# Clearing the semaphores of each stage inside the following stage instead of in a step of its own

## What is computed

```python
x = _layernorm(x + _L0_gnn_ref(x, edge_index, W1, b1, W2, b2))          # two graph convolutions
x = _layernorm(x + _L1_gnn_ref(x, edge_index, edge_type_8, W, root, bias))  # mean for each of 8 edge types
x = _layernorm(x + _L2_gnn_ref(x, W, edge_index, edge_type_8))          # attention, softmax over an edge type
x = _layernorm(x + _L3_gnn_ref(x, weight, edge_index, edge_type_16))    # sum for each of 16 edge types, relu
```

## Time and profile before

| | us |
|---|---|
| median of 3 runs | 3187.77 |
| lowest, highest | 3186.46, 3187.91 |
| profiled execution, its time | 3188.55 |
| profiled execution, span from first to last instruction | 3186.8 |
| mean granted TensorE clock in it | 0.854 |
| busy PE, DVE, ACT, POOL | 2283.0, 2338.2, 1719.3, 2111.0 |

### The profile page before, as it was taken

The page is one execution under the profiler, slowest core; times in us unless marked ns, Lnnn a source line. Parts: engine busy times, 40 slices in busy tenths (PEclk is TensorE's granted clock), DMA queues, the critical chain, the costliest instruction groups (busy, mean ns, idle before and its releaser), DMA issues. The chain is left out here.

```text
span 3186.8 us, 51629 instructions
## 1 busy us (share of the span) xinstructions
PE 2283.0 (72%) x9863; PEld 1461.5 (46%) x9864; DVE 2338.2 (73%) x7354; ACT 1719.3 (54%) x4736; POOL 2111.0 (66%) x2070
## 2 busy tenths in 40 slices
PE   2666661777746666599999576577645499999996
PEld 1444441666645666344444333366534355444442
DVE  7999982788859889599999211133489678899996
ACT  1776892898947777466666344455458512121221
POOL 1777776777547777477776677577540277677775
PEclk9998996999978788799999699755555599999998
DMA  1666672455536666355554587799745423222221
GB/s 49 216 214 199 205 219 75 151 177 172 167 108 188 192 184 186 118 148 150 151 157 148 174 269 267 223 284 288 232 128 175 138 70 73 63 60 62 62 63 38
DMA packets 320188, 497.19 MB, mean 156 GB/s; under 512 B 65930, under 2 KB 144681, under 8 KB 320058
## 3 DMA queue, kind: packets, MB, share of 16 engines
q1 hardware_dynamic: 251130, 379.68, 37.3%
q0 software_dynamic: 68928, 116.12, 13.8%
HBM read 262.91 MB, written 236.52 MB: 157 GB/s over the span
## 5 line engine op out<-in xcount | busy, mean ns | idle before, releaser
L2156 PE MATMUL bank<-sum_masked,sum_w 128*128 128x512 f32 x1280 | 568.5, 596 | 6.7 <-DVE sum_masked L2215 6.7
L2215 DVE SCALAR_TENSOR_TENSOR sum_masked<-sum_typ,sum_col 128x512 f32<-128x512 bf16 x640 | 401.5, 684 | 21.0 <-ACT sum_col L2131 17.5
L1381 PE MATMUL bank<-mean_masked,mean_w 128*128 128x512 f32 x784 | 376.7, 612 | 18.7 <-DVE mean_masked L1472 18.7
L2156 PEld LDWEIGHTS bank<-sum_masked,sum_w 128*128 128x128 f32 x1280 | 236.5, 191 | 281.3 <-issue 210.1
L2075 POOL DMA_INDIRECT sum_rows<-t_x,m_row_int x160 | 171.7, 1073 | 197.2 <-POOLq L122 148.8
L2097 POOL DMA_INDIRECT out_dram<-sum_new,m_last_int x196 | 220.9, 1127 | 88.0 <-issue 57.8
L1237 POOL DMA_INDIRECT mean_rows<-t_x,m_row_int x196 | 213.8, 1091 | 95.5 <-issue 95.5
L1472 DVE SCALAR_TENSOR_TENSOR mean_masked<-mean_typ,mean_col 128x512 f32<-128x512 bf16 x392 | 250.0, 680 | 20.8 <-ACT mean_col L1317 20.7
L1237 POOL DMA_INDIRECT c_rows<-t_g,m_row_int x196 | 188.7, 963 | 109.7 <-issue 56.7
L1698 POOL DMA_INDIRECT at_xs<-t_x,at_order x204 | 193.6, 949 | 94.3 <-issue 60.7
L1248 POOL DMA_INDIRECT order<-m_row_int,m_order_int x196 | 213.0, 1087 | 59.7 <-issue 59.7
(11 more groups left out here) (366 smaller groups left out, 6039.0 us busy)
## 6 DMA issues: line engine op xcount, KB each, us to landing
t_hu<-at_made SPq DMA_DIRECT2D x51, 512.0 KB, 3.7
pf_xc<-x_dram SPq DMA_DIRECT2D x98, 256.0 KB
t_g<-pf_g SPq DMA_DIRECT2D x98, 256.0 KB
t_x<-pf_x SPq DMA_DIRECT2D x98, 256.0 KB
c_dense_x<-t_x SPq DMA_DIRECT2D x98, 256.0 KB, 3.8
t_x<-c_dense_x SPq DMA_DIRECT2D x98, 256.0 KB
c_same<-p_same SPq DMA_DIRECT2D x98, 128.0 KB, 3.5
t_g<-c_new SPq DMA_DIRECT2D x49, 256.0 KB
```

Source lines behind the costliest of these rows:

```text
L1381: pe.matmul(H[q][:, :], w[:, r, :], masked[:, r % MASKS, :], start=(r == 0), stop=(r == n_rel - 1))\
L2156: pe.matmul(H[n % 2][:, :], w[:, r * D:(r + 1) * D], masked[:, r % 8, :], start=(r == 0), stop=(r == R16 - 1)).then_inc(mask_used, 1)
L2215: v.scalar_tensor_tensor(out=masked[:, r % 8, :], in0=typ[:, n % 2, :], scalar=float(r), in1=col[:, n % 2, :], op0=ALU.is_equal, op1=ALU.m ...
```

## The change

The second Block behind each stage goes. A stage's exit now calls `finish`, which emits no instruction: it gives back the semaphores of the stage before (already cleared by then) and notes its own as `m.finished`. Each following stage has `clear_finished(pool, m)` in GpSimd's list. One Block with `clear_finished` stands behind sum.

```diff
-    def clear(self):
-        with self.nc.Block() as block:
-            @block.gpsimd
-            def _(pool):
-                for s in self.mine:
-                    pool.sem_clear(s)
-        for s in self.mine:
+    def finish(self, m):
+
+        for s in m.finished:
             self.nc.release_semaphore(s)
+        m.finished = self.mine
+
+
+def clear_finished(pool, m):
+
+    for s in m.finished:
+        pool.sem_clear(s)
...
-        ctx.callback(sem.clear)
+        ctx.callback(sem.finish, m)
         block = ctx.enter_context(nc.Block())
...
+            clear_finished(pool, m)
             with pool.If(out_of_order(pool)):
...
+
+        @block.gpsimd
+        def _(pool):
+            clear_finished(pool, m)
...
                 gather_info(pool, m, k)
+            clear_finished(pool, m)
             hold(pool, gathered, KT * 16)
             hold(pool, m.info_gathered, (KT - INFO_LATE) * 16)
...
+            clear_finished(pool, m)
             if kind == ATTEND:
                 for z in range(KZ):
...
+            clear_finished(pool, m)
             for q in range(4):
                 pool.wait_ge(scattered[q], of_four(NB - 1 - (NB - 1 - q) % 4, q, 16 * BT))
...
     m = Memory()
+    m.finished = []
...
         sum_stage(nc, io, m)
+        with nc.Block() as block:
+            @block.gpsimd
+            def _(pool):
+                clear_finished(pool, m)
```

## The result

The kernel after takes 3158.89 us (median of 5 runs, 3155.18 to 3161.65), the kernel before 3187.72 on the same chip (5 runs, 3185.77 to 3187.91). The ratio is 0.9911, with an interval of 0.9897 to 0.9925: 28.8 us less, where 22.4 were forecast.

A forecast was written before the change was run, and what follows sets the result against it. No engine is busy over 73%, so eleven stages run in a row, with clearing steps in series between them. 3187.77 - 22.4 for ten steps, moved clears and late starts at 0, gives 3165.4 us; 8-in-10 range 3162.8 to 3173.4.

The forecast's parts named there:

- The removed steps: Ten of the eleven clearing steps between two barriers behind the stages go, saving their full length, 22.4 us.
- The count of clears: Cross-check of the ten steps: 288 clears at 0.065 us plus ten drains and barriers at 0.3 us, together 21.7 us.
- The clears at nothing: 288 clears moved into GpSimd's lists in the stages add 0 us; upper bound 2.3 us.
- The rival in which clears wait for the DMAs: Clears queue until GpSimd's DMAs are worked off, in attention and sum: 2.3 us given back, 3167.7; chance 0.05.
- What is late next: Start of the next stage's list behind each barrier: 0 us taken, at most 2.0 to 3.5 us for one boundary.
- the rivals in which the steps were cover for code: Boundaries stall on code loads: four give back 8 to 14 us, chance 0.13; all ten cost 35 us, chance 0.03.
- The argument against code loads: In prefill's step nobody stopped for the instruction load there, as the 38 clears kept their pitch.
- the range's lower end: Whole kernel: 3162.8 us, from known executions of the kernel before lying 2.1 us below.

The follow-up runs named there:

- empty_step: The kernel after with the ten second Blocks put back without their clears, each one drain and one barrier: 3167.93 us, ratio 0.9932 to the kernel before.
- pool_first: The kernel after with prefill's 12 clears at the head of GpSimd's list instead of behind the gathers: 3163.53 us.
- pool_pad12: The kernel after with 12 drains added to GpSimd's list in setup: 3167.89 us.
- second set: Both kernels run again unaltered: the kernel after 3160.75 us against 3189.18 for the kernel before, ratio 0.9912.
- dve_pad18: The kernel after with 18 drains at the head of VectorE's list in ATTEND: 3166.06 us, one run.
- before_ranges: The kernel before, second Blocks kept, with each step's clears written as clears of semaphore ranges, 26 instructions instead of 313: 3168.84 us, ratio 0.9937.
- pool_pad21: The kernel after with 21 drains added to GpSimd's list in setup: 3154.28 us, one run.

## Why the prediction was right, and where it was short

- **The removed steps: right.** 22.4 us were forecast, 22.26 measured. The count of clears (21.7) was the worse of the two ways, as it put a barrier at 0.3 us; empty_step shows 0.33.
- **The clears at nothing: right, by the reason given.** The sequencer runs ahead: sum's 37 clears were over at 3142.2, when GpSimd still had 6 us of scatters to do; the drain behind them took 4.615 us, against 4.625. The rival in which clears wait for the DMAs, 2.3 us, is out. In attention, where I gave it 1.8 us of cover, the stage is as long as before within its scatter (532.2 and 531.7 against 532.1 and 530.3).
- **What is late next: right for the ten boundaries, and too narrow a question.** SP's first load comes 0.07 us behind the release that is left at eight boundaries and 0.26 behind that of constants, as it did before; softmax has none. So the rivals in which the steps were cover for code, 8 to 35 us back, are out, although one such wait can be made: pool_first and pool_pad12 have 3.6 and 3.7 us. I asked this only as a possible cost ("bounded from below by nothing"). The value below nothing was excluded by the sentence that every boundary starts as prefill's does. It doesn't: the trace of before had GpSimd's first gather of prefill 2.3 us behind the release, with 1.45 us of "issue" in front, while behind prefill's own barrier and step the first gather came 0.8 us behind the release. The argument against code loads, that the 38 clears of prefill's step kept their pitch, was misread too: in the rows of setup, prefill, attention and ATTEND one gap is 0.36 to 0.44 us instead of 0.07, each with an instruction packet 0.7 us behind it.
- **The step that failed is the range's lower end, with the term "what is late next" held at nothing or more.** In its place the runs show 6.5 us (6.2 in the second set) that the stages themselves became shorter. The lower end was made of the scatter of before alone, 2.1 us, and even that was subtracted wrongly: 3165.4 - 2.1 is 3163.3 and not 3162.8. What it left out is that the removal shortens each engine's list, and that the trace of before holds waits that depend on the place in it or change for another reason. I had read the longest "issue" waits on VectorE and ScalarE, as a price for new ones; the same view has one of 4.8 us on GpSimd, in the stage that GpSimd bounds:

```profile
POOL m_xd L614 <- issue: 65.4, 196, 4.8
```

- **The excess, by its parts.** Of 6.5 us between the medians prefill gave 3.3 (4.3 in the second pair of profiled executions), VectorE's loop branch in ATTEND 8 x 0.21 = 1.7, and MEAN's passes 8 x 0.08 = 0.6: 5.6. The remaining 0.9 lies within the runs' scatter, and so does much of the sum, which only the medians give and not each pair of traces. That ATTEND's part is the place of VectorE's code is shown by dve_pad18, and by empty_step and before_ranges, which leave VectorE's list as long as before and have before's pass. That the first gather depends on the place of GpSimd's code is shown by pool_first, pool_pad12 and pool_pad21; it is 1.3 of prefill's 3.3 us. The other 2 us of prefill and MEAN's 0.6 are measured, but their cause isn't known.
- **What stays open.** Why the wait ahead of the 114th gather takes one of three lengths (4.4, 4.9 and 5.8 us from start to start) isn't settled. It follows neither the other engines' code nor the number of Blocks nor the place in GpSimd's code, and no packet of instructions moves ahead of it. Nor is it known what shortened MEAN's pass: it is 34.37 us where the ten Blocks stand and 34.29 where they don't. And empty_step had before's prefill length with after's first gather: 1.5 us of it are the 114th's wait, the rest is not placed.
- **Scatter.** Sets of seven runs of the kernel before span 4.3 to 5.5 us, sets of four and five of the kernel after 4.4 and 6.5. Three runs within 1.5 us and the profiled one were too few to take the range's lower end from.

## What to carry to other kernels

Here a step between two barriers cost its full length, and the wait of an engine that had no work in it measured it. Clears queued on an engine that had to wait for its DMAs anyway added nothing, and where they can't be moved a range clear took most of their cost away in place. When an edit changes the number of instructions ahead of later loops, look in the trace for waits called "issue" on the engine that bounds each stage, the first instruction behind each boundary and the loop branches among them, and let the range reach to both sides by their size. A few us won or lost that way belong to no line of the diff: read them by stage lengths, against a second execution of each kernel.

## What the runs showed of the hardware

- A loop's branch on VectorE cost by the place of the loop in its code: 0.90 us against 0.69 from the last normalisation to the next pass's scan, with identical instructions. All fourteen profiled executions show 0.89 to 0.92 or 0.68 to 0.69 at the seven crossings behind the first, and 1.17 or 0.71 at the first.
- GpSimd waited 3.6 to 3.7 us ahead of its 62nd executed instruction in the two kernels in which that was a gather with nothing queued ahead of it, even where it had stood idle for 46 us in setup, with the padding's drains done. With clears at that place there is a gap of 0.44 us in their row, and behind a row of queued gathers nothing can be seen of it. In pool_pad12 two packets of the instruction queue lie between 60 and 63 us, in the kernel after one, and the second at 66.6.
- The Trainium skill (Runtime: NRT & Kernel Launch, section "Instruction fetch mechanics") says that code is fetched ahead in order, in blocks of 16 KiB, mostly hidden, and that a taken branch to a page that isn't in the window stalls. No boundary here shows such a stall behind the removed steps. The wait of 3.7 us at the 62nd instruction speaks against "mostly hidden" for straight code, if it is a fetch, as the packet 2.0 to 2.3 us ahead of the gather suggests.
- A barrier over five engines with nothing to wait for takes 0.33 us. A clear takes 38 ns, 0.06 to 0.07 us from start to start, behind queued gathers and scatters as behind a drain; a clear of a range took 47 to 220 ns.
